# Two transformer layers on one core: the first MLP product of each layer's first chunk placed inside the last two attention steps

## The reference

```python
mod = silu(condition) @ Wada + bada
sh_a, sc_a, gt_a, sh_m, sc_m, gt_m = split(mod, 6, axis=1)
xm = layernorm(x, g1, be1) * (1.0 + sc_a[:, None, :]) + sh_a[:, None, :]
x = x + gt_a[:, None, :] * attention(xm, Wqkv, Wproj, bproj)
xm = layernorm(x, g2, be2) * (1.0 + sc_m[:, None, :]) + sh_m[:, None, :]
h = gelu(xm @ W1 + b1, approximate=False)
x = x + gt_m[:, None, :] * (h @ W2 + b2)
```

## Time and profile before

| | |
|---|---|
| median of 3 runs | 1156.61 us (1155.13 to 1156.92) |
| profiled execution | 1153.95 us, its span 1152.1 us |
| TensorE busy (share of the span) | 1073.7 us (93%) |
| VectorE busy | 786.7 us (68%) |
| ScalarE busy | 620.1 us (54%) |
| GpSimd busy | 252.4 us (22%) |
| mean granted TensorE clock | 0.97 of full |

### The profile page before, as it was taken

The page is one execution under the profiler, slowest core; times in us unless marked ns, Lnnn a source line. Parts: engine busy times, 40 slices in busy tenths (PEclk is TensorE's granted clock), DMA queues, the critical chain, the costliest instruction groups (busy, mean ns, idle before and its releaser), DMA issues.

```text
span 1152.1 us, 24600 instructions
## 1 busy us (share of the span) xinstructions
PE 1073.7 (93%) x8972; PEld 939.3 (82%) x8972; DVE 786.7 (68%) x2379; ACT 620.1 (54%) x1255; POOL 252.4 (22%) x253
## 2 busy tenths in 40 slices
...
PEclk9689999999999999999996999999999999999999
...
DMA packets 50833, 81.52 MB, mean 71 GB/s; under 512 B 8917, under 2 KB 23477, under 8 KB 49621
## 3 DMA queue, kind: packets, MB, share of 16 engines
...
...
## 4 chain that ended last, share of the span: by engine, by line
PE 83%; DMA 5%; DVE 4%; ACT 2%; SPq 2%; issue 2%; POOL 2%; ACTq 0%; POOLq 0%; DVEq 0%
PE g_bank L564 14%; PE st_bank L564 14%; PE o_bank L652 9%; PE o_bank L564 7%; PE s_bank L564 7%; PE s_bank L619 6%; PE st_bank L638 5%; PE st_bank L632 4%; PE s_bank L615 3%; PE st_bank L634 3%; PE g_bank L710 2%; DMA k_stack<-qk_split 2%; SPq L423 2%; DMA q_stack<-negmaxT 2%; PE g_bank L718 1%
## 5 line engine op out<-in xcount | busy, mean ns | idle before, releaser
L833 ACT ACTIVATE probs<-st_bank 128x384 f32<-128x384 f32 (+1 forms) x512 | 273.5, 548 | 145.1 <-PE st_bank L634 78.6
L936 ACT ACTIVATE probs<-st_bank,cols 128x512 f32<-128x512 f32 x128 | 87.9, 688 | 214.5 <-PE st_bank L564 188.5
L564 PE MATMUL st_bank<-qk_split,q_stack 128*128 128x512 f32 x768 | 187.4, 402 | 15.8 <-ACT probs L936 11.2
L1129 DVE CUSTOM_DVE_ANT_0 s_bank<-s_bank,tri_wide 128x128 f32<-128x128 f32 (+1 forms) x512 | 170.4, 387 | 36.0 <-PE s_bank L616 34.7
L1135 DVE TENSOR_REDUCE maxima<-s_bank 128x2 f32<-128x512 f32 x256 | 168.8, 685 | 35.4 <-PE s_bank L619 34.6
L564 PEld LDWEIGHTS st_bank<-qk_split,q_stack 128*128 128x128 f32 x768 | 144.8, 191 | 53.5 <-ACT probs L936 14.7
L652 PE MATMUL o_bank<-probs,v_sb 128*32 128x256 f32 (+1 forms) x2048 | 124.9, 362 | 1.6 <-ACT probs L833 1.6
L564 PE MATMUL g_bank<-xmT,wa 128*128 128x256 f32 x768 | 121.7, 298 | 4.9 <-POOL xmT L1313 4.8
L619 PE MATMUL s_bank<-k_stack,q_stack 97*128 97x256 f32 x512 | 116.7, 313 | 3.8 <-DVE maxima L1135 1.9
L638 PE MATMUL st_bank<-q_stack,k_stack 99*128 99x256 f32 x512 | 104.5, 288 | 11.0 <-DMA q_stack<-negmaxT 10.2
L1313 POOL TENSOR_TENSOR xmT<-xm_full,xmT 128x512 fp32r<-128x512 f32 x32 | 42.3, 1323 | 329.9 <-ACT xmT L899 329.9
...
## 6 DMA issues: line engine op xcount, KB each, us to landing
...
```

Source lines behind the costliest of these rows:

```text
L564: last = mm(dst, weights[i], rows[j], start=(f == 0 and n == 0), stop=(f == tiles - 1 and n == len(TERMS) - 1))
L833: activation(probs[:, h % 8, 0:n], st_bank[h % 2][:, 0:n], ACT.Exp, scale=SCALE)\
L936: activation(h_full[:, m % 2], st_bank[m % 2][:, :], ACT.Gelu, bias=cols[:, cb + m:cb + m + 1])\
L1129: last = v.tensor_tensor_reduce(out=bank[:, keys], in0=bank[:, keys], in1=tri_wide[:, T - (i + 1) * P:T], scale=1.0, scalar=LOWEST, op0=AL ...
```

## The change

For each layer:

- Step 16: VectorE makes chunk 0's statistics in slot 3 and its normalised rows in slot 7, GpSimd its deviation.
- Step 17: ScalarE casts W1 tile by tile in slots 4 to 11, GpSimd subtracts (before: VectorE).
- Step 18: TensorE transposes chunk 0 in slot 1, ScalarE modulates it in slots 2 and 3, VectorE makes the low half in slots 3 and 4 and casts W2 in slots 4 to 7 (before: ScalarE), GpSimd subtracts for W2. Hidden tiles 0, 1 and 2 are made in slots 9, 11 and 13. Chunk 1's statistics stand in slot 13.
- Step 19: hidden tiles 3 to 7 in slots 4, 6, 7, 9 and 10, the gelus in slots 4 to 11, their splits one slot later, chunk 1's normalised rows in slot 7.
- Chunk 0's hidden tiles use five banks (`s_bank` 0 to 2, `st_bank` 0 and 1) in turn, its gelus and modulated rows lie in `v_sb` 1 and 0.
- The load of layer 1's MLP weights is issued in step 6 of layer 1. The load of layer 1's projection weights waits for chunk 0's last split; their cast is in `mlp_step` 2 and their subtraction on GpSimd at the start of `mlp_step` 3.

```diff
+        H_SLOT = {(B + 2, 9): 0, (B + 2, 11): 1, (B + 2, 13): 2, (B + 3, 4): 3, (B + 3, 6): 4, (B + 3, 7): 5,
+                  (B + 3, 9): 6, (B + 3, 10): 7}
+        G_SLOT = {(B + 3, 4 + m): m for m in range(NM)}
...
+        def h_bank(b, m):
+            return (s_bank + st_bank)[m % 5] if b.const == 0 else st_bank[m % 2]
...
-                    if layer == 0 and t.const == 14:
-                        load_mlp_weights(0)
+                    if t.const == (14, 6)[layer]:
+                        load_mlp_weights(layer)
...
-                    sp.wait_ge(o_copied, NG * B)
-                    sp.dma_start(wa_raw[1], wa_in[1]).then_inc(wa_loaded, 16)
...
+                        if c.const == 0:
+                            sp.wait_ge(o_copied, NG * B)
+                            sp.wait_ge(m_xmT, 2)
+                            sp.wait_ge(m_hT, NM)
+                            sp.dma_start(wa_raw[1], wa_in[1]).then_inc(wa_loaded, 16)
...
-                    load_mlp_weights(1)
...
-                    if s == SLOT["xT"] and t.const == ATTN_END:
+                    if s == 1 and t.const == ATTN_END - 1:
                         chunk_transposes(layer, Step(0))
+                    if (t.const, s) in H_SLOT:
+                        hidden(layer, Step(0), H_SLOT[t.const, s])
...
+            def hidden(layer, b, m):
+                gb = b - (-NCH * layer)
+                first = b.const == 0
+                if m == 0:
+                    pe.wait_ge(m_xmT, gb.count(2, 2))
+                if first:
+                    pe.wait_ge(w1_split, NM * layer + m + 1)
+                if first and m in (3, 4):
+                    pe.wait_ge(exp_done, H * B * (layer + 1) - (4 - m))
+                elif first:
+                    wait(pe, m_gelu, gb.count(NM, m - 4) if m >= 5 else None)
+                else:
+                    wait(pe, m_gelu, gb.count(NM, m - 1))
+                bank = h_bank(b, m)
+                for f in range(NF):
+                    last = product(bank[:, :], [w1[:, e, f, m * P:(m + 1) * P] for e in range(2)],
+                                   [xmT_m[:, e, f, :] for e in range(2)], f, NF)
+                last.then_inc(m_h, 1)
...
+                    if t.const == ATTN_END - 2 and 4 <= s < 4 + NM:
+                        m = s - 4
...
+                        activation(w1[:, 0, :, at], w1_raw[:, :, at], ACT.Copy).then_inc(w1_high, 1)
+                    if t.const == ATTN_END - 1 and s in (2, 3):
+                        chunk_modulated(layer, Step(0), (s - 2,))
+                    if (t.const, s) in G_SLOT:
+                        gelu(layer, Step(0), G_SLOT[t.const, s])
...
-                if layer == 0 and t.const == 1:
+                if layer == 0 and t.const == 2:
                     act.wait_ge(proj_ready, B)
                     act.wait_ge(wa_loaded, 32)
...
-                for m in range(NM):
-                    at = slice(m * P, (m + 1) * P)
-                    activation(w1[:, 0, :, at], w1_raw[:, :, at], ACT.Copy).then_inc(w1_high, 1)
-                for m in range(NM):
-                    activation(w2[:, 0, m], w2_raw[:, m], ACT.Copy).then_inc(w2_high, 1)
...
+                    if t.const == ATTN_END - 3 and s == 3:
                         chunk_statistics(layer, Step(0))
...
+                    if t.const == ATTN_END - 1 and s in (3, 4):
+                        chunk_low(layer, Step(0), (s - 3,))
+                    if t.const == ATTN_END - 1 and 4 <= s < 8:
...
+                        for m in (2 * s - 8, 2 * s - 7):
+                            v.tensor_copy(w2[:, 0, m], w2_raw[:, m]).then_inc(w2_high, 1)
+                    if (t.const, s - 1) in G_SLOT:
+                        split_hidden(layer, Step(0), G_SLOT[t.const, s - 1])
+                    if t.const == ATTN_END - 1 and s == 13:
+                        chunk_statistics(layer, Step(1))
+                    if t.const == ATTN_END and s == 7:
+                        chunk_normalise(layer, Step(1), range(CT))
...
+                if t.const == ATTN_END - 2:
+                    for m in range(NM):
+                        at = slice(m * P, (m + 1) * P)
+                        pool.wait_ge(w1_high, NM * layer + m + 1)
+                        g_.tensor_tensor(w1[:, 1, :, at], w1_raw[:, :, at], w1[:, 0, :, at], ALU.subtract)\
+                            .then_inc(w1_split, 1)
+                if t.const == ATTN_END - 1:
                     for m in range(NM):
                         pool.wait_ge(w2_high, NM * layer + m + 1)
                         g_.tensor_tensor(w2[:, 1, m], w2_raw[:, m], w2[:, 0, m], ALU.subtract).then_inc(w2_split, 1)
...
+                if layer == 0 and t.const == 3:
+                    for f in range(NF):
+                        pool.wait_ge(wa_high, 2 + f)
+                        g_.tensor_tensor(wa[:, 1, f], wa_raw[1][:, f], wa[:, 0, f], ALU.subtract).then_inc(wa_split, 1)
```

109 lines of the change are left out of this document (52 added, 57 removed).

## The result

| | before | after |
|---|---|---|
| median of 5 runs | 1156.61 us (1155.13 to 1157.18) | 1143.94 us (1142.95 to 1145.22) |
| profiled execution, its span | 1153.95, 1152.1 | 1142.95, 1141.2 |
| mean granted clock | 0.970 | 0.968 |
| ratio | | 0.9878, 95% interval 0.9854 to 0.9903 (the two medians alone give 0.9890) |

The change wins 12.7 us, where 19.9 were forecast: 1143.94 us lies inside the range of 1130 to 1146 and outside the forecast's own 1132 to 1142.

A forecast was written before the change was run, and what follows sets the result against it. TensorE is busy nearly everywhere, so only its waits and slow clock can be won. 8.6 + 7.3 - 2 x 0.5 - 2 x 0.5 + 6.0 = 19.9 us less gives 1136.7 us, own range 1132 to 1142, wider range 1130 to 1146.

The forecast's parts named there:

- Behind the last exponential: Attention's end, step 19: second product starts 14.5 us after the last exponential; net 8.6 us less in layer 0, 7.3 in layer 1.
- 0.5 a layer: Step 19: charge for a lower clock behind TensorE's 2.5 us wait, 0.5 us a layer, bounds 0 and 1.7.
- Into step 18: Three early hidden products (4.3 us) and ScalarE's modulations (1.9) move the last exponential 6.2 us later, 5.5 in layer 1.
- W2's casts: Step 18: VectorE keeps its turn against GpSimd, eight casts end some 2 us after they begin; cost nothing.
- rival A: Step 18: GpSimd gets the port between W2's casts, which take some 8 us; 4 us a layer, 1145 us; chance 0.12.
- Steps 16 and 17: Chunk 0's statistics and normalisation, W1's casts and subtractions beside a full TensorE: 0.5 us a layer, bounds 0 and 2.
- Attention weights' split: Layer 1's attention-weight subtractions on GpSimd move from chunk 1 to chunk 2: moved, not saved, 0, bounds -1 and +2.
- The passage: Between the layers: without the MLP weight load, wait shrinks by about 5.1 us plus 0.9 clock; 6.0 less, bounds 3 and 9.
- B: Rival: the passage does not gain, because restacking and constant rows fill the DMA engines anyway; 1142.7 us; chance 0.10.
- C: Rival: more is won, row of maxima lands at once, clock holds, step 18's exponentials catch up; 1131 us; chance 0.09.
- E: Rival: early products wait for W1's low half or modulated rows, step 18 grows as step 19 shrinks; 1150 us; chance 0.05.
- D: Rival: clock falls to 1.2 GHz from step 18 through the second product, costing 25 us a layer; 1187 us; chance 0.03.

The follow-up runs named there:

- experiment 2: Changed kernel plus nine unread matmuls filling TensorE's wait in step 19 of each layer: 1142.42 us, ratio 0.9876 to the kernel before.
- experiment 9: Changed kernel with unread matmuls filling four TensorE waits of each layer, in steps 17, 18 and 19: 1137.86 us, ratio 0.9824 to the kernel before.
- experiment 1: Changed kernel with the load of layer 1's MLP weights put back at the passage between the layers: 1146.37 us, ratio 0.9909 to the kernel before.
- experiment 3: Changed kernel with GpSimd's subtractions of W2 starting only after all eight casts: 1146.16 us, ratio 0.9914 to the kernel before.
- experiment 4: Changed kernel with GpSimd's two attention-weight subtractions spread over chunks 2 and 3, each behind a gated sum: 1139.79 us, ratio 0.9858 to the kernel before.
- experiment 6: Changed kernel with ScalarE's modulations of step 18 in slots 3 and 6, VectorE's low halves in 4 and 7: 1144.20 us, ratio 0.9892 to the kernel before.
- Experiment 5: Changed kernel with step 19's attention output ahead of chunk 1's normalisation and the eighth hidden product behind the transposes: 1141.24 us, ratio 0.9873 to the kernel before.
- experiment 7: Kernel before with only the load of layer 1's MLP weights moved to step 6 of layer 1: 1155.61 us, ratio 0.9971 to the kernel before.

## Why the prediction was right in direction and its gain over half too large

**Behind the last exponential (forecast -8.6 and -7.3).** The mechanism held: one table load, a first gelu at E + 2.0, VectorE's list setting the pace, a wait of 2.5 before the output weights. The second product starts at E + 16.1 and E + 16.6 instead of 14.5 and 14.6. At the full clock, with the wait filled, it starts at E + 14.6 and E + 14.7 (experiments 2 and 9), so the sum over the engines' lists held to 0.1 us. The step that failed is "**0.5 a layer**" for the clock behind this wait: experiment 2 measures it at 1.5 and 2.7, 4.2 us against 1.0. It isn't a fixed price: in the five kernels with this wait open (the changed one, 1, 3, 4 and 6) behind took 23.31 to 26.05 us in layer 0 and 25.18 to 26.43 in layer 1, so 0 to 2.8 more than with the wait filled, 2.0 on average. In the prediction the bounds of 0 and 1.7 came from the two cases of the earlier trace rows, one with and one without a low clock, and I took a value near a third of the upper end; layer 1 went beyond it. And the wait itself was treated as given, though it hung on the place of 1.38 us of normalisation on VectorE's list. Experiment 5 takes it away, and its clock with it: 6.2 us.

**Into step 18 (forecast +6.2 and +5.5).** Measured +7.3 and +8.5. The term that was mis-sized is the "**1.9**" for ScalarE's modulations. They stand exactly where TensorE has nothing but scores to do, which run no more than two heads ahead. With the modulations in slots 3 and 6 the step is +6.0 in layer 0 (experiment 6), with a wait of 1.20 left; in slots 2 and 3 it is 1.2 more whether the clock is low (22.12) or full (22.09, experiment 9). In layer 1 the clock comes on top: 23.73 with a low stretch of 7 us, 22.43 with filled waits, 21.41 with the modulations moved as well, where the forecast's +5.5 makes 20.7. So of its excess of 3.0, 1.3 is clock and 1.7 the modulations and products. (The unread matmuls may themselves take up to 0.4 of these: in layer 0, 0.96 of them and a wait of 0.27 stand for a wait of 0.83.)

**W2's casts (0; rival A 8).** The sentence "VectorE kept its turn", from one row where GpSimd's instruction was the one that waited, did not carry over. Once the first subtraction had started, one cast ended for each subtraction:

```profile
376.71 4.96 DVE L1208 CAST q_stack<-wm_f32r 128x256 fp32r<-128x256 f32 x8
```

```profile
377.08 5.88 POOL L1375 TENSOR_TENSOR q_stack<-wm_f32r,q_stack 128x256 fp32r<-128x256 f32 x8 [5.49 <-DVE q_stack L1208]
```

Eight casts in 4.96 us instead of 2, at the pace of GpSimd's subtractions, 5.88/8 = 0.74, and not at the sum of both durations that rival A had put (8 us). GpSimd lost little: its eight took 5.55 alone (experiment 3). That VectorE's cast has to wait for GpSimd's instruction agrees with the exclusive lock that the Trainium skill describes (SBUF — State Buffer, "SBUF: two separate sides"). That the lock is held for the whole instruction doesn't fit these rows: a cast and a subtraction would then take 0.29 + 0.73 = 1.02 us, and they took 0.74. TensorE saw 0.41 of it. The forecast's "Cost nothing" was right within that: experiment 3 lets the casts run alone and gains nothing. Rival A had the order of the two engines right and a price that was far too high.

**Steps 16 and 17 (+0.5 a layer).** Step 16 is the same to 0.01 us, so chunk 0's statistics and normalisation cost nothing there. W1's casts and subtractions in step 17 cost nothing that can be told either. Without TensorE's wait for the row of maxima, and at the same length of low clock, layer 0's step takes 17.35 us in the kernel before and 17.37 in experiment 6, and 18.93 in experiment 7 (the old step) against 18.96 in the changed kernel. Its +1.6 is how long the clock stayed low behind that wait, which is in the kernel before as well; its -1.0 in layer 1 is a full clock, some 1.4, against a wait that was 0.4 longer. The 0.5 was right on average for the wrong reason.

**Attention weights' split (0).** Moved, not saved, at -3.8 and +5.1: +1.2, inside the bounds of -1 and +2. The 1.2 is again clock: in experiments 1 and 6, where none falls in chunk 2, chunks 2 to 4 take 74.19 and 74.23, just the 3.8 more that chunk 1 takes less. The prediction took this cost as given; experiment 4 shows that all 5.1 can be had.

**The passage (-6.0).** -7.0 in the two profiles, 4.9 alone (experiment 7), 5.8 by putting it back (experiment 1), 4.4 as a mean of all kernels. The sum had the wait go from 7.30 to 2.2; it went to 0.34 (0.42 in experiment 7), but another appeared at the next restacking (2.73 and 3.38), which was not in the sum. By the mean of all kernels the forecast was about 1.6 too large, which chance hid in the profile: behind these waits the clock was low for 10 us in the kernel before and for 3 to 7 in most others, and not at all in the changed kernel's profile.

**The load's new place.** 0.4 in the step whose end is layer 1's fourth y_sb (20.16 to 20.57), 0.1 in experiment 7, up to 0.8 in the other kernels; within the bound of 2, and not the nothing of the sum.

**Start-up.** +1.2 before anything that the change touches, chance. The profiled executions differ by 11.0 and the medians by 12.7, so 1.7 of the difference is from the choice of executions.

Of the rivals B, C and E did not occur: the passage gained, the early products never waited for W1 or the rows, and no more was won than forecast. D's mechanism, a low clock behind the new waits, did occur, not as one that stays over 50 us but as stretches of 3 to 10 us.

**The signs.** The order of things came out as the prediction said, the sizes of its signs mostly not: the second product came 16.1 and 16.6 us after the last exponential and not 14 to 15, step 18 grew by 7.3 and 8.5 and not 5 to 7, the wait at the passage was 0.34 and not 1 to 3, and the pair of waits came back as one. The sign of rival A, casts with means over 0.5 us, did show. So the measured time lies beside A's 1145 and B's 1142.7, and inside the range because that takes them in; that is chance, for neither mechanism made it: A's cost TensorE 0.41 us and not 4 a layer, and the passage did gain.

The missing 9.0 us are then: 3.2 clock behind step 19's wait, 1.3 clock in layer 1's step 18, 1.2 clock in chunk 2, -0.4 in the two steps 17, 2.8 in the two steps 18 from the modulations and products (1.1 and 1.7), 1.2 start-up, 0.6 along layer 1's attention, -1.0 passage: 8.9. Over half, 5.7, is clock that the forecast had as small change. The largest part of the clock and of the modulations is shown by experiments 1, 2, 6 and 9; the split of layer 1's 1.7 between modulations and products stays open.
